# Two message passes read their softmax weights from PSUM, and the mixing product shares the pairs' three banks

## What is computed

```
scores = leaky(h_src . attn_src + h_dst . attn_dst)
w      = exp(scores - amax[dst]);  w = w / denom[dst]
out    = segment_sum(h_src * w, dst)
```

## Time and profile before

| | |
|---|---|
| median of three executions | 2983.78 us (2980.12 to 2986.76) |
| the profiled execution's own time | 2979.18 us |
| its span | 2977.4 us |
| busy: PE, DVE, ACT, POOL | 2298.1, 1399.9, 1059.5, 1403.0 us |
| first pass (`attend`): first gather, end of the stage | about 359 us, 916 us |
| pass between: first and last gather | 1660 us, 2154 us |
| last pass (`aggregate`): first gather, end of the stage | about 2204 us, 2731 us |

### The profile page before, as it was taken

The page is one execution under the profiler, slowest core; times in us unless marked ns, Lnnn a source line. Parts: engine busy times, 40 slices in busy tenths (PEclk is TensorE's granted clock), DMA queues, the critical chain, the costliest instruction groups (busy, mean ns, idle before and its releaser), DMA issues. The chain is left out here.

```text
span 2977.4 us, 42673 instructions
## 1 busy us (share of the span) xinstructions
PE 2298.1 (77%) x11382; PEld 1713.3 (58%) x11382; DVE 1399.9 (47%) x3453; ACT 1059.5 (36%) x2811; POOL 1403.0 (47%) x1426
## 2 busy tenths in 40 slices
PE   3899737766677988999994697876745988774996
PEld 3465324444445767888883465554534777553775
DVE  6655426666666230111115332342257666555677
ACT  2422224444442112332332443265412565442320
POOL 2122377777750042111110577777767777774300
PEclk8999858778888899999997898988865999997998
DMA  6256544444421014676663433343556444434001
GB/s 196 81 161 202 159 113 113 115 115 116 113 78 31 1 64 142 203 219 199 217 200 108 152 105 106 105 136 114 168 168 187 125 128 126 123 111 150 33 0 44
DMA packets 244440, 374.17 MB, mean 126 GB/s; under 512 B 66889, under 2 KB 179861, under 8 KB 244235
## 3 DMA queue, kind: packets, MB, share of 16 engines
q0 software_dynamic: 64624, 179.69, 21.0%
q1 hardware_dynamic: 132718, 140.75, 15.5%
q10 hardware_dynamic: 46892, 51.32, 5.2%
HBM read 301.77 MB, written 69.88 MB: 125 GB/s over the span
## 5 line engine op out<-in xcount | busy, mean ns | idle before, releaser
L2668 POOL DMA_INDIRECT cm_rows<-rows,e_bsrc x392 | 373.9, 954 | 202.5 <-issue 97.5
L1403 POOL DMA_INDIRECT at_rows<-values,e_brow x392 | 391.9, 1000 | 139.8 <-issue 92.0
L1132 POOL DMA_INDIRECT store<-rows,e_bsrc x392 | 397.3, 1013 | 119.5 <-issue 104.5
L1479 PE MATMUL at_part<-at_msg,store 128*128 128x265 f32 x880 | 272.5, 453 | 85.0 <-DVE at_msg L1634 49.9
L2804 PE MATMUL cm_part<-cm_rows,cm_one 128*128 x880 | 261.9, 440 | 91.9 <-SPq L2680 61.5
L1157 PE MATMUL banks<-ag_msg,ag_one 128*128 128x258 f32 x880 | 236.2, 405 | 85.6 <-issue 43.3
L2804 PEld LDWEIGHTS cm_part<-cm_rows,cm_one 128*128 128x128 f32 x880 | 180.2, 217 | 157.8 <-issue 133.9
L1479 PEld LDWEIGHTS at_part<-at_msg,store 128*128 128x128 f32 x880 | 179.1, 220 | 157.3 <-DVE at_msg L1634 81.4
L3019 DVE TENSOR_TENSOR store<-store,cm_part 128x256 f32 x220 | 92.2, 419 | 336.2 <-PE cm_part L2804 308.2
L1157 PEld LDWEIGHTS banks<-ag_msg,ag_one 128*128 128x128 f32 x880 | 167.1, 198 | 139.2 <-issue 55.7
L2105 POOL DMA_INDIRECT expert_out<-x_y,x_target x56 | 53.7, 959 | 370.5 <-DVE x_y L2208 363.1
(11 more groups left out here) (660 smaller groups left out, 3988.5 us busy)
## 6 DMA issues: line engine op xcount, KB each, us to landing
x_w<-in_L_ffn_W1p SPq DMA_DIRECT2D x32, 1024.0 KB, 5.2
x_w<-in_L_ffn_W2p SPq DMA_DIRECT2D x32, 1024.0 KB, 5.6
values<-p_hv ACTq DMA_DIRECT2D x25, 1088.0 KB, 4.9
p_brow<-local_row SPq DMA_DIRECT2D x44, 320.0 KB, 3.5
xn_acc<-low_row SPq DMA_DIRECT2D x28, 448.0 KB
expert_in<-z_z POOLq DMA_DIRECT2D x7, 1032.0 KB
je_y<-expert_out SPq DMA_DIRECT2D x25, 256.0 KB, 2.8
at_rows<-values,e_brow POOLq DMA_INDIRECT x392, 2.8
```

Source lines behind the costliest of these rows:

```text
L1132: pool.indirect_dma_start(rows[:, b % slots, k, :], None, table, bass.IndirectOffsetOnAxis(index[:, k, b:b + 1], 0)).then_inc(gathered[b % ...
L1403: pool.indirect_dma_start(rows[:, b % RING, k, :], None, table, bass.IndirectOffsetOnAxis(e.block_row[:, k, b:b + 1], 0)).then_inc(gathere ...
L1479: last = pe.matmul(part[:, n % deep, 0:wide], one[:, n // U % 2, k, n % U, :], msg[:, n % 4, k, :], start=(k == 0), stop=(k == K2 - 1))
L2668: pool.indirect_dma_start(rows[:, b % SLOTS, k, :], None, table, bass.IndirectOffsetOnAxis(e.block_src[:, k, b:b + 1], 0)).then_inc(gather ...
```

## The change

Four things, with their code.

1. In `aggregate`, the product L1193 takes its weight from PSUM: `segment_softmax` has PE transpose channel 0 of the exponentials a second time, into the bank `small` (K2 more transposes for each half of the blocks), and returns that bank as `factors`. ACT's copy `scores` stays, and L1192 still reads it.
2. In `attend`, the product L1634 reads its weights straight from `turn`. ACT's copy to `at_w` (14 of them) and the semaphore `w_kept` go; `back_turned` takes its place in DVE's waits. `turn` gets two banks, used by odd and even chunks.
3. The second bank for `turn` was that of `mix`: the mixing product now takes its turn in the three banks of `part`, in one order with the pairs. A product or a pair waits (`bank_free`) until the item three before it in that order has been added by DVE.
4. PE's wait before it writes `turn` is now on `weighted` for the chunk two before.

```
@@ segment_softmax, PE, before the transposes of half h
+                for k in range(K2):
+                    pe.transpose(small[:, k * NB + h * BH:k * NB + (h + 1) * BH], s[:, h, 0, k * P:(k + 1) * P], c.ident[0:BH, 0:BH])
...
+    return (back_kept, len(steps)), turn, small[:, 0:K2 * NB].rearrange("p (k b) -> p k b", k=K2)
@@ aggregate, DVE
-                    dve.tensor_tensor(msg[:, n % 4, :, 0:D], row, w[:, :, 0:1].broadcast_to([P, K2, D]), ALU.mult).then_inc(weighted, 1)
+                    dve.tensor_tensor(msg[:, n % 4, :, 0:D], row, factors[:, :, bass.ds(b, 1)].broadcast_to([P, K2, D]), ALU.mult).then_inc(weighted, 1)
@@ attend, order of the banks
+    for n in range(G):
+        taken += ([("mix", mix_at[n])] if n in mix_at else []) + [("pair", n)]
+    bank = {what: i % deep for i, what in enumerate(taken)}
+    held = {what: taken[i - deep] for i, what in enumerate(taken) if i >= deep}
...
-        w = m_.sb("at_w", [P, 2, K2, CH, H0])
...
-        mix = m_.ps("at_mix", [P, 512])
-        turn = m_.ps("at_turn", [P, 512])
+        turn = m_.ps("at_turn", [P, 2, 512])
@@ attend, PE
+            def bank_free(what):
+                if what in held:
+                    kind, at = held[what]
+                    pe.wait_ge(summed if kind == "pair" else mix_added, at + 1)
...
                     if pc:
-                        pe.wait_ge(w_kept, pc)
                         pe.wait_ge(shifted, pc)
+                    if pc >= 2:
+                        pe.wait_ge(weighted, CHUNKS[pc - 1][0])
...
-                    if t:
-                        pe.wait_ge(mix_added, t)
+                    bank_free(("mix", t))
...
-                if n >= deep:
-                    pe.wait_ge(summed, n - deep + 1)
+                bank_free(("pair", n))
@@ attend, ACT
-                if i == 4:
-                    if pc >= 2:
-                        act.wait_ge(weighted, CHUNKS[pc - 1][0])
-                    act.wait_ge(back_turned, pc + 1)
-                    act.copy(w[:, pc % 2, :, 0:m, :].rearrange("p k n h -> p k (n h)"),
-                             turn[:, 0:K2 * q].rearrange("p (k q) -> p k q", k=K2)).then_inc(w_kept, 1)
@@ attend, DVE, weigh
                 if j == 0:
-                    dve.wait_ge(w_kept, pc + 1)
+                    dve.wait_ge(back_turned, pc + 1)
+                many = CHUNKS[pc][1]
+                w = turn[:, pc % 2, 0:K2 * many * H0].rearrange("p (k n h) -> p k n h", k=K2, n=many)[:, :, j, :]
...
-                                  w[:, pc % 2, :, j, :].unsqueeze(3).broadcast_to([P, K2, H0, HW]), ALU.mult).then_inc(weighted, 1)
+                                  w.unsqueeze(3).broadcast_to([P, K2, H0, HW]), ALU.mult).then_inc(weighted, 1)
```

More of the change, by code:

```diff
@@ L1099, in _, with aggregate @@
                     dve.tensor_tensor(s[:, h], fwd[:, h, 0:1, :].broadcast_to([BH, 2, BLK]), s[:, h], ALU.subtract).then_inc(shifted, 1)
-    return (back_kept, len(steps)), turn
+    return (back_kept, len(steps)), turn, small[:, 0:K2 * NB].rearrange("p (k b) -> p k b", k=K2)
 SLOTS = 14
 LAG = 5
-def aggregate(nc, tag, c, e, index, table, heads, weights, acc, ring, banks, gate, ride):
+def aggregate(nc, tag, c, e, index, table, heads, weights, factors, acc, ring, banks, gate, ride):
     width = table.shape[1]
@@ L1356, in attend @@
     mix_at = {8 * t + 4: t for t in range(NT)}
+    taken = []
+    for n in range(G):
+        taken += ([("mix", mix_at[n])] if n in mix_at else []) + [("pair", n)]
+    bank = {what: i % deep for i, what in enumerate(taken)}
+    held = {what: taken[i - deep] for i, what in enumerate(taken) if i >= deep}
     first = {lo: pc for pc, (lo, m) in enumerate(CHUNKS)}
@@ L1365, in attend @@
             preset, copied, scored, sloped, leaked, scanned, tipped, taken, reset, raised, carried, sorted_, spread_out,
-            carry_kept, spread, shifted, exped, back_turned, w_kept, ended, gaps, gap_made,
+            carry_kept, spread, shifted, exped, back_turned, ended, gaps, gap_made,
             faded, fade_kept, rescaled, biased, mixed, mix_added, x_in0, x_in1, x_in2, *gathered):
@@ L1426, in softmax @@
                         for k in range(K2):
-                            last = pe.matmul(turn[0:q, k * P:(k + 1) * P], of[:, k].rearrange("p n h -> p (n h)"), c.ident[:],
+                            last = pe.matmul(turn[0:q, pc % 2, k * P:(k + 1) * P], of[:, k].rearrange("p n h -> p (n h)"), c.ident[:],
                                              start=(n == 0 and k == 0), stop=(n == 1 and k == K2 - 1))
@@ L1454, in softmax @@
                     for k in range(K2):
-                        last = pe.transpose(turn[:, k * q:(k + 1) * q], s[0:q, k * P:(k + 1) * P], c.ident[0:q, 0:q])
+                        last = pe.transpose(turn[:, pc % 2, k * q:(k + 1) * q], s[0:q, k * P:(k + 1) * P], c.ident[0:q, 0:q])
                     last.then_inc(back_turned, 1)
@@ L1467, in _ @@
                     t = mix_at[n]
-                    if t:
-                        pe.wait_ge(mix_added, t)
+                    bank_free(("mix", t))
                     for k in range(DC):
-                        last = pe.matmul(mix[:, 0:D], xnt[:, k, t * P:(t + 1) * P], g[:, k, :], start=(k == 0), stop=(k == DC - 1))
+                        last = pe.matmul(part[:, bank["mix", t], 0:D], xnt[:, k, t * P:(t + 1) * P], g[:, k, :], start=(k == 0), stop=(k == DC - 1))
                     last.then_inc(mixed, 1)
@@ L1475, in _ @@
                 pe.wait_ge(weighted, n + 1)
-                if n >= deep:
-                    pe.wait_ge(summed, n - deep + 1)
+                bank_free(("pair", n))
                 for k in range(K2):
-                    last = pe.matmul(part[:, n % deep, 0:wide], one[:, n // U % 2, k, n % U, :], msg[:, n % 4, k, :], start=(k == 0), stop=(k == K2 - 1))
+                    last = pe.matmul(part[:, bank["pair", n], 0:wide], one[:, n // U % 2, k, n % U, :], msg[:, n % 4, k, :], start=(k == 0), stop=(k == K2 - 1))
                 last.then_inc(multiplied, 1)
@@ L1518, in softmax @@
                         act.wait_ge(leaked, pc)
-                    act.activation(slope[0:q, :], turn[0:q, 0:BLK], ACT.Copy, scale=SLOPE).then_inc(sloped, 1)
+                    act.activation(slope[0:q, :], turn[0:q, pc % 2, 0:BLK], ACT.Copy, scale=SLOPE).then_inc(sloped, 1)
                 if i == 3:
@@ L1565, in softmax @@
                     if pc:
-                        dve.wait_ge(w_kept, pc)
+                        dve.wait_ge(back_turned, pc)
                         dve.wait_ge(ended, pc)
                     dve.wait_ge(sloped, pc + 1)
-                    dve.tensor_tensor(s[0:q, :], slope[0:q, :], turn[0:q, 0:BLK], ALU.max).then_inc(leaked, 1)
+                    dve.tensor_tensor(s[0:q, :], slope[0:q, :], turn[0:q, now, 0:BLK], ALU.max).then_inc(leaked, 1)
                     dve.wait_ge(spread_out, pc + 1)
@@ L1647, in add_up @@
                 dve.wait_ge(multiplied, n + 1)
-                dve.tensor_tensor(acc[:, tile, :], acc[:, tile, :], part[:, n % deep, 0:wide], ALU.add).then_inc(summed, 1)
+                dve.tensor_tensor(acc[:, tile, :], acc[:, tile, :], part[:, bank["pair", n], 0:wide], ALU.add).then_inc(summed, 1)
             dve.memset(xin[:, 2, :], 0.0).then_inc(preset, 1)
@@ L1675, in _ @@
                     dve.tensor_tensor(xnt[:, :, t * P:(t + 1) * P], xin[:, t % 2 if t < NT - 1 else 2, :].rearrange("p (k f) -> p k f", k=DC),
-                                      mix[:, 0:D].rearrange("p (k f) -> p k f", k=DC), ALU.add).then_inc(mix_added, 1)
+                                      part[:, bank["mix", t], 0:D].rearrange("p (k f) -> p k f", k=DC), ALU.add).then_inc(mix_added, 1)
                 if n >= 2:
@@ L3476, in program @@
                     made = score2(nc, c, e, tgt, own, firsts, starts, low_row, s2, source, banks, shared)
-                    gate, down_ps = segment_softmax(nc, "sm2_", c, e, 1, 2, s2, source, scores, banks, *made)
-                    aggregate(nc, "ag2_", c, e, e.block_src, rows2, 1, scores, acc, store[:], banks, gate,
+                    gate, down_ps, factors = segment_softmax(nc, "sm2_", c, e, 1, 2, s2, source, scores, banks, *made)
+                    aggregate(nc, "ag2_", c, e, e.block_src, rows2, 1, scores, factors, acc, store[:], banks, gate,
                               MlpRide(RIDDEN, xnt_rows, x_rows, ACT.Gelu, weights, down_ps, gate))
```

2 lines of the change are left out of this document (1 added, 1 removed).

## The result

The changed kernel takes **2945.22 us** (median of 4 executions, 2942.35 to 2948.67); the kernel before, beside it on the same chip, 2982.08 us. The ratio is 0.9875 with a 95% interval of [0.9858, 0.9892]: faster. The profiled execution took 2942.35 us, its span is 2940.5.

A forecast was written before the change was run, and what follows sets the result against it. Gathers on POOL were taken to bound the first and last passes. Terms -37.1 + 1.1 - 0.4 + 1 = -35.4 us take the profiled 2979.2 to 2943.8, or 2948 us on the median's scale; range 2938 to 2970.

The forecast's parts named there:

- The holder: First and last pass: a DVE instruction with two SBUF inputs holds gathers that begin under it; removing this gains 37.1 us.
- The rival "nothing changes": Both passes: the product as such isn't the holder and one PSUM operand changes nothing; 2984 us, chance 0.07.
- First pass: First pass: the product's holds cost 18.9 us of gather time, of which 17.7 us reach the stage's end.
- -0.4 for `at_w`: First pass, tail: ACT's copy of the weights goes, shortening one 2.2 us wait by 0.4 us.
- the +1.1: Both passes: freed gathers start at other moments and can meet holding instructions that stay; 1.1 us given back.
- Last pass: Last pass: 19.4 us of gather time lost to the product, all of it reaching the end.
- Product's own length: Both products: a broadcast read from PSUM costs 0; bounds -1 us in all and 0.45 us more a product (then 2974).
- Mixes: First pass: the mixing product's new waits in part are covered except for two in the tail, 0 to 3.4 us, taken as 1.
- Waits for a block in the last pass: Last pass, DVE: waits for blocks would fall to about 50 us, from 70.2 after 2500 us.
- Slack of 6.2 us a chunk: First pass: DVE waits 7.75 us a chunk for gathers, less 1.5 for faster gathers, leaving 6.2 us of slack.
- The slower rival: Products: repeated PSUM reads take two cycles an element, +0.56 us a product, making DVE the first pass's bound; 2998 us, chance 0.06.
- One pass only: First pass: POOL runs into the full ring or DVE's softmax paces it; only the last pass gains, 2965 us, chance 0.12.

The follow-up runs named there:

- the middle pair of experiments: Changed kernel plus a useless product ahead of each sum in the pass between, with two SBUF operands (2982.25 us) or one in PSUM (2973.73 us).
- banks_only: Kernel before, with only the mixing product moved to take its turn in the part banks: 2983.22 us, ratio 1.0006.
- the full one: Changed kernel plus a second, full-size product (128x528, one PSUM operand) ahead of each first-pass product: 3016.95 us, ratio 1.0109.
- dose_half: Changed kernel plus a second product of half size (128x264, one PSUM operand) ahead of each first-pass product: 2983.56 us, ratio 1.0006.
- middle_one_psum: Changed kernel plus a useless 384-element product, one operand in PSUM, ahead of each sum in the pass between: 2973.73 us, ratio 0.9967.

## Why the prediction was right, and where its steps were off

Predicted were 2948.0 us, measured 2945.2, and by the mechanism that was named. Step by step:

- **The holder** was named rightly: two SBUF inputs. The held gathers fell to none (131 of 161 before, by the count above), and the middle pair of experiments shows the same by one operand alone. The rival "nothing changes", with the remark of the Trainium skill (page "SBUF — State Buffer", section "Who interferes with whom") that `tensor_tensor` leaves the making of descriptors alone, is out by the trace: for these indirect gathers it doesn't.
- **First pass**, -17.7 for the product, -0.4 for `at_w`, +1 for the mixes and some of the +1.1: -16.8 at the stage's end. The mean is 950 ns, as forecast.
- **Last pass**, -19.4 plus its part of the +1.1: -20.5. The mean is 961 ns where 965 was forecast; freed gathers met fewer other instructions than the term for them assumed (L1337 holds 4, where the same line held 12 before).
- **Product's own length**, 0: it is 4 ns shorter. The bound of +0.45 us, the rival's +0.56, and the 65 ns that the prediction's estimate by the Trainium skill (page "VectorE: DVE Perf Modes", section on the TRN2 errata) would add are all not there.
- **Mixes**, +1: `banks_only` has +1.8 at the stage's end, in one execution, and -1 to +5 us by its interval: not contradicted, not measured.
- **Waits for a block in the last pass**, "about 50": missed, 31.6. The step that failed took the saving straight off the waits for blocks (70.2 less 19.4). But DVE runs into the gathers later now: before, it had waited 15.2 us for blocks by 2540 us, 336 us after the pass's first gather; now, by the same 2540 us, 352 after it, it has waited 2.0. The ring that PE works off lasts longer when it is refilled faster. Its waits for PE and issue, 84.0 us together where they were 68.8, take part of the place. That the fuller ring accounts for the rest I infer; no run tests it. The pass still ends when the gathers let it, so the time wasn't touched.
- **Slack of 6.2 us a chunk**: mis-sized, and the reading beneath it was wrong. I took DVE's 7.75 us wait as waiting for gathers. Of a dose of 6.8 us a chunk 4.1 were absorbed, and moving ACT's matrices gave back 24 to 28 us of the full one. The shorter waits were forecast well (85.2 us in 11 waits became 69.6, 1.4 each), because gathers did pace the stretch between; what they didn't pace is the queue on ACT ahead of each chunk and behind the last one. The slower rival was therefore nearer than the text had it: it turned at 0.49 us a product there, while `dose_half`, with 0.43 us, had already used up the whole gain. Nothing of the forecast hung on it, because the product didn't grow.
- **One pass only**, by a full ring: out, with two slots fewer nothing is lost.

## What to carry to other kernels

When equal instructions have a median at their minimum and a mean above it, pair the long ones with what runs on the other engines, by start times; here a free change of one operand's memory was worth 1.2%. Don't take an engine's wait for slack before the chain behind it is read: here a good part of it was another engine's program order, and putting the short urgent step ahead of the long block of work gave 9 us more. Nor is idle time summed over a pass slack in each of its stretches. And to price a wait, add a known dose of work and see how much of it comes through.

## What the runs showed that I had not expected

- The hold depends on the instruction, not on DVE being busy, and two SBUF operands aren't the only form that holds. In the changed kernel the bfloat16 `tensor_scalar` of 128 x 1792 in the last pass (L2518), with one SBUF tensor, holds 12 of the 13 gathers that begin under it, 3.8 us in all, and under the `tensor_reduce` of 128 x 350 (L2529) 8 of 12 are lengthened, by 0.5 us in all. The copies of 128 x 4 (L1194), SBUF to SBUF, hold none of 21.
- A product of 0.55 us on an engine that waits 300 us of its pass for others cost 28 us there (`middle_one_psum`), all but a few in one stretch of 137 us: 6.8 us of waits and 23.7 us of PE at a lower granted clock.
- Two slots of the ring, 5 us of gathers, made no difference to either the changed kernel or the dosed one.
